# Two cross-attention layers on one core: the probability product in one run, two-chunk steps and a third context buffer in the masked layer

## The chip, the cores and the metric

The kernel runs on one core of one Trainium2 chip. The metric is the device time of that core in microseconds (us), and lower is better. Most executions of one kernel agree within 0.3%.

## The reference

A gated decoder block with two layers works on 32 batches of 56 query tokens (width 128), which attend to 1500 context rows each. Cut to what matters:

```python
x = x + tanh(g_xattn[0]) * diff_attention(layernorm(x), ctx, ctx, ...)  # 32 heads of 4, softmax(q k) v, a1 - lam * a2, rms per head
x = x + tanh(g_ffn[0])   * moe_ffn_0(layernorm(x))                       # 8 experts, top 2, and a shared one
x = x + tanh(g_xattn[1]) * attention(layernorm(x), ctx, ctx, mask, ...)  # 16 heads of 8, masked keys
x = x + tanh(g_ffn[1])   * moe_ffn_1(layernorm(x))                       # 8 gated experts, top 2
```

Only the two attention layers are touched by the change.

## The kernel before

`attend` (L490) runs once per layer: layer 0 (`L0`, 32 heads, no mask) and layer 1 (`L1`, 16 heads, mask). The 32 batches follow one another. The 1500 keys of a batch are cut into 12 chunks of 125 keys, and the kernel takes one **step** per chunk. All engines have an order written out by hand, in which the batches overlap: while batch n is weighed, the maximum is searched for n+1 and n+2, values are projected for n+2, and keys for n+3 (`LEAD`).

On TensorE (PE) a step holds these pieces of work.

- **Scores**, `scores` (L941): keys against queries of one chunk into the PSUM tensor `score_ps[0]` or `[1]` (two banks each). In layer 0 a step has two halves of 896 columns, "place 0" and "place 1", and each half has its own `score_ps`. The halves swap places from step to step (`halves_of`), so that place 0 of a step uses the same `score_ps` as place 1 of the step before. In layer 1 a chunk has 896 columns in all, and the chunks alternate between the two; two matmuls at L962 put the mask in first.
- **Pairs**, `search` (L927): two matmuls of 112 x 500 scores, from which VectorE (DVE) takes a row maximum (`reduce_piece`, L1119). They rotate through three PSUM rooms: `spare_ps`, `max_ps[0]`, `max_ps[1]`. Layer 0 has 48 pieces in a batch (two pairs a step), layer 1 has 24 (one pair a step).
- **The product**, `weigh` (L973): probabilities times values into `acc_ps`, as eight float32 matmuls of 32 output partitions each; four stand side by side in the array. It works on the step before. In layer 0 it is split into two halves of four, with other work between them, except at step 0. In layer 1 the two halves stand together.
- **Preparations**, `use` (L883): T (turn the context), K (project a third of the keys), V (project a third of the values), M (turn the maxima), F and A (turn the output and its normalised form). The table `where` gives the step of each. In layer 0 they write into the `score_ps` that place 0 of the step has used; in layer 1 they take their turn in the three rooms of the pairs.

The order in a step of layer 0 is scores 0, pair 0, scores 1, first half of the product, pair 1, preparation, second half. In layer 1 it is scores, pair, product, preparation. A preparation is copied out by ScalarE (ACT, `drain`, L1038; M of layer 1 by DVE). ACT also takes the exponential of each 125 x 896 scores (`exps`, L1069) and copies the output of a batch out (`copy_output`, L1078).

**SyncE (SP)** issues all transfers, in this order for batch n:

```python
fill_k(n + 2)      # L682: 6 loads of key parts into the key stack of n+2
load_q(n + 3)      # L660: 6 small loads
next_mask(n + 3)   # L712, layer 1
next_context(n + 4)
fill_m(n + 1)      # L693: 4 small transfers of the split maxima, after M
store_k(n + 3)     # L676: 2 stores of the projected keys, from khl to k_parts
```

`fill_k` waits for the two stores of its batch to land and for the scores of the batch that used the slot (three slots). The context of layer 1 has two buffers (`context_parts`, L303), and `next_context` waits until the values of batch n+2 are projected. The search of batch n+2 begins five steps before the end of batch n (`AHEAD`).

**GpSimd (POOL)**: `prepare` (L763) builds the query stack and turns the mask into the two forms that the scores (`mask_f`) and the search (`mask_add`) need; `finish` (L810) normalises the output; `split_keys` (L799) splits the projected keys into two float16 parts.

Of the kernel before, what the change touches and what calls it, by code (L numbers as in the profile page):

```python
# [48 lines left out]
class Layer:  # L49

    def __init__(self, name, heads, hd, masked):
# [12 lines left out]
        self.uses_f = 2  # L64
# [55 lines left out]
def build(nc, a, out):  # L120

    ctx = ExitStack()
    with ctx:
# [132 lines left out]
        for L in (L0, L1):  # L256
            T[f"{L.name}_mask_loaded"] = sem(f"{L.name}_mask_loaded")
            T[f"{L.name}_context_loaded"] = [sem(f"{L.name}_context_loaded{i}") for i in range(1 + L.masked)]
# [44 lines left out]
def context_parts(T, i):  # L303

    return T["ctx_f"][:, i, 0:SK].bitcast(F16).rearrange("p (a k) -> p a k", a=2)


def load_context(sp, T, L, n):

    loaded = T[L.name + "_context_loaded"]  # L310
    if L.masked:
        sp.dma_start(context_parts(T, n % 2), T["ctx_dram"][n:n + 1, :, :, :].rearrange("b d a k -> (b d) a k")).then_inc(loaded[n % 2], 16)
# [177 lines left out]
def attend(T, L):  # L490
# [14 lines left out]
    GD, GC, H = L.group_dims, L.group_cols, L.halves  # L505
# [7 lines left out]
    ctxT = [context_parts(T, 0), context_parts(T, 1) if L.masked else  # L513
            T["kstack"][2][:, K_WORDS:K_WORDS + 2 * SK].rearrange("p (a k) -> p a k", a=2)]
# [41 lines left out]
    LAST, LAST_THIRD = NKT - 1, NTHIRD - 1  # L556
# [11 lines left out]
    if L is L0:  # L568
        where = {("T", 0): (1, 1), ("F", 0): (2, 1), ("T", 1): (3, 1), ("F", 1): (4, 1), ("T", 2): (5, 1), ("K", 0): (6, 1),
                 ("M", 0): (7, 1), ("V", 0): (7, 1), ("K", 1): (8, 1), ("V", 1): (9, 1), ("K", 2): (10, 1), ("A", 0): (11, 1),  # L570
                 ("V", 2): (11, 1)}
# [6 lines left out]
    per_step = L.pieces // NKT  # L578
    assert per_step * NKT == L.pieces
    AHEAD = 5  # L580
    early = AHEAD * per_step
    turnaround = [("F", i) for i in range(L.uses_f)] + [("A", 0)]
# [8 lines left out]
    def at_step(n, t, side):  # L591

        return [(kind, n + LEAD[kind], i) for (kind, i), place in where.items()
                if place == (t, side) and 0 <= n + LEAD[kind] < B]

    def searched(n, t, k):


        if 2 * k >= per_step:
            return []  # L600
        d, place = (1, early + t * per_step) if t < NKT - AHEAD else (2, (t - NKT + AHEAD) * per_step)
# [4 lines left out]
    for n in range(B):  # L606
        for t in range(NKT):
            middle, last = at_step(n, t, 1), at_step(n, t, 2)
            spare_uses += middle + last
            if H == 2:  # L610
                in_scores.update({user: n * NKT + t for user in middle})
                middle = []
            order += searched(n, t, 0) + middle + searched(n, t, 1) + last
# [6 lines left out]
    def halves_of(step):  # L620

        return (0, 1) if step % 2 == 0 or H == 1 else (1, 0)

    def room(user):
# [3 lines left out]
        if user in in_scores:  # L628
            return score_ps[halves_of(in_scores[user])[0]][:, int(user[0] in "MA"), :]
# [15 lines left out]
    with nc.Block() as block:  # L645

        @block.sync
        def _(sp):
# [23 lines left out]
            def store_context(n):  # L672
                sp.wait_ge(s_cp, low_part(n, LAST_THIRD))
                sp.dma_start(T["ctx_dram"][n:n + 1, :, :, :].rearrange("b d a k -> (b d) a k"), ctxT[n % 2]).then_inc(s_cst, 16)
# [7 lines left out]
            def fill_k(n):  # L682
                at_least(sp, s_scores, (n - 2) * NKT * H)
# [18 lines left out]
            def next_context(n):  # L702
# [3 lines left out]
                if L.masked:  # L706
                    at_least(sp, s_v, NTHIRD * (n - 1))
# [797 lines left out]
```

## Time and profile before

| what | value |
|---|---|
| median of 3 runs | 2349.78 us (2349.38 to 2350.72) |
| profiled execution, its own time | 2345.43 us |
| its span, first to last instruction | 2343.1 us |
| mean granted TensorE clock | 0.953 |
| PE busy | 2179.4 us (93%) |
| PE weight loads | 1297.5 us (55%) |
| DVE busy | 1677.4 us (72%) |
| ACT busy | 1507.4 us (64%) |
| POOL busy | 1278.7 us (55%) |
| DMA | 227.82 MB, mean 97 GB/s |

The attention of layer 0 runs from about 140 to 1220 us, that of layer 1 from about 1480 to 2170 us; between and behind them are the feed-forward layers. PE is busy nearly all of the time in both attention layers, but a busy PE is not PE at its peak: matmuls overlap, and the end of each is modelled. So the cost of a piece of work is read here from start to start: the start of the next piece less its own.

### The profile page before, as it was taken

The numbers are of one execution on the slowest core, as the hardware profiler recorded it, in microseconds if no ns is written. First come the engines' busy times: TensorE is split into PE (matmuls) and PEld (weight loads), VectorE is DVE, ScalarE is ACT, GpSimd is POOL, SyncE is SP. The second block draws the span as 40 slices with busy tenths as digits, with TensorE's granted clock in tenths as the row PEclk, the third lists the DMA queues.
The fourth block names the chain that finished last, engine by engine and source line by source line (L and its number), as shares of the span: only waits on it lengthen the run. The fifth ranks groups of instructions, "written<-read, shape, count | busy, mean of one in ns | idle before, by whom it ended". The sixth has DMA issues, their size and how long they took to land. (4 is left out here: it accounts for less than half of the span.)

```text
span 2343.1 us, 67447 instructions
## 1 busy us (share of the span) xinstructions
PE 2179.4 (93%) x27256; PEld 1297.5 (55%) x27256; DVE 1677.4 (72%) x3701; ACT 1507.4 (64%) x2133; POOL 1278.7 (55%) x1418
## 2 busy tenths in 40 slices
PE   3799999999999999999976967999999999999798
PEld 2255555555555555555535853666665666666576
DVE  3688888888888888888825455777776677775644
ACT  2177787787787787787773322677676667667322
POOL 5335555555655655655423445677776777772332
PEclk9599999999999999999997985999999999999799
DMA  3635344344344344344201018576665666661100
GB/s 102 130 75 117 89 100 115 89 103 114 88 103 113 94 100 111 97 98 110 48 2 64 24 35 158 126 143 148 137 140 128 136 137 138 146 124 36 55 1 16
DMA packets 95245, 227.82 MB, mean 97 GB/s; under 512 B 46308, under 2 KB 58852, under 8 KB 88292
## 3 DMA queue, kind: packets, MB, share of 16 engines
q1 hardware_dynamic: 94692, 223.67, 42.3%
q8 instruction: 210, 3.44, 0.7%
q14 instruction: 87, 0.71, 0.1%
q10 hardware_dynamic: 256, 0.00, 0.0%
HBM read 146.77 MB, written 76.48 MB: 95 GB/s over the span
## 5 line engine op out<-in xcount | busy, mean ns | idle before, releaser
L1075 ACT ACTIVATE probs<-score_ps 125x896 f32<-125x896 f32 x1152 | 1014.2, 915 | 203.3 <-PE score_ps L968 200.9
L1133 DVE TENSOR_REDUCE max_part<-max_ps 112x1 f32<-112x500 f32 x1024 | 654.3, 668 | 115.2 <-PE spare_ps L937 66.9
L984 PE MATMUL acc_ps<-probs,vext 125*32 125x224 f32 (+1 forms) x12288 | 670.7, 316 | 2.7 <-issue 2.1
L937 PE MATMUL max_ps<-kstack,qstack 48*112 48x500 f16 x1535 | 507.1, 405 | 4.7 <-DVE max_part L1133 2.6
L968 PE MATMUL score_ps<-qstack,kstack 50*125 50x224 f16 (+1 forms) x6144 | 453.6, 243 | 15.7 <-ACT probs L1075 13.9
L968 PEld LDWEIGHTS score_ps<-qstack,kstack 50*125 50x125 f16 x6144 | 343.1, 134 | 181.1 <-issue 120.2
L1130 DVE CUSTOM_DVE_ANT_0 kstack<-max_ps,kstack 112x500 f32<-112x500 f32 x511 | 335.2, 675 | 127.1 <-PE max_ps L937 75.0
L1133 DVE TENSOR_REDUCE max_part<-spare_ps 112x1 f32<-112x500 f32 x512 | 343.1, 670 | 64.3 <-PE max_ps L937 64.3
L984 PEld LDWEIGHTS acc_ps<-probs,vext 125*32 125x32 f32 x12288 | 260.8, 109 | 220.1 <-issue 151.0
L937 PE MATMUL spare_ps<-kstack,qstack 48*112 48x500 f16 x769 | 310.0, 403 | 19.2 <-issue 15.8
L937 PEld LDWEIGHTS max_ps<-kstack,qstack 48*112 48x112 f16 x1535 | 173.2, 128 | 142.7 <-issue 77.7
L806 POOL CAST khl<-kstack 128x500 f16<-128x500 f32 x189 | 112.9, 598 | 226.7 <-ACT kstack L1054 143.9
L1130 DVE CUSTOM_DVE_ANT_0 kstack<-spare_ps,kstack 112x500 f32<-112x500 f32 x257 | 173.5, 675 | 87.2 <-PE max_ps L937 75.2
L808 POOL TENSOR_TENSOR khl<-kstack,khl 128x500 f16<-128x500 f32 x189 | 201.8, 1068 | 15.3
L1459 POOL TENSOR_TENSOR kstack<-kstack,probs 112x512 f32 (+1 forms) x68 | 90.5, 1331 | 171.3 <-DVE probs L1406 171.2
L823 POOL TENSOR_TENSOR heads_out<-turned,rden 56x64 f32<-56x64 f32 x192 | 55.2, 288 | 216.9 <-DVE rden L1116 206.8
L962 PE MATMUL score_ps<-kstack 56*125 56x448 f16 x768 | 157.8, 401 | 0.2 <-issue 0.2
L777 POOL TENSOR_SCALAR kstack<-mask_in 112x1500 bf16<-112x1500 uint8 x31 | 147.1, 4746 | 2.6
L774 POOL TENSOR_SCALAR kstack<-mask_in 120x1500 f16<-120x1500 uint8 x31 | 147.6, 4762 | 0.0
L937 PEld LDWEIGHTS spare_ps<-kstack,qstack 48*112 48x112 f16 x769 | 98.7, 128 | 82.1 <-issue 60.4
L1058 ACT ACTIVATE vext<-score_ps 125x512 f32<-125x512 f32 x102 | 60.9, 597 | 76.7 <-PE score_ps L911 76.2
L766 POOL TENSOR_TENSOR qstack<-qrows,wide 112x896 f16<-112x896 f16 (+1 forms) x64 | 83.5, 1305 | 47.0 <-DMA qrows<-q_parts 24.8
(200 smaller groups left out, 2688.3 us busy)
## 6 DMA issues: line engine op xcount, KB each, us to landing
kstack<-k_parts SPq DMA_DIRECT2D x384, 187.5 KB, 6.6
k_parts<-khl SPq DMA_DIRECT2D x128, 375.0 KB, 2.7
ctx_f<-in_ctx SPq DMA_DIRECT2D x32, 750.0 KB
ctx_f<-context_parts SPq DMA_DIRECT2D x32, 750.0 KB, 4.5
context_parts<-ctx_f SPq DMA_DIRECT2D x16, 750.0 KB, 3.7
context_parts<-kstack SPq DMA_DIRECT2D x16, 750.0 KB, 3.5
mask_in<-in_mask SPq DMA_DIRECT2D x128, 82.0 KB
qrows<-q_parts SPq DMA_DIRECT2D x384, 7.0 KB, 7.0
```

The lines of the kernel that those rows point to most:

```text
L774: nc.gpsimd.tensor_scalar(by_chunk(mask_f[n % SLOTS][0:HALF + SQ, :]), turned_keys(mask_in[0:HALF + SQ, :]), -BIG, None, ALU.mult).then_in ...
L777: nc.gpsimd.tensor_scalar(by_chunk(mask_add[n % SLOTS]), turned_keys(T["mask_in2"][:, :]), -BIG * BIG, None, ALU.mult).then_inc(s_add, 1)
L806: nc.gpsimd.tensor_copy(khl[:, 0, k], key_f[:, k]).then_inc(s_kp, 1)
L808: nc.gpsimd.tensor_tensor(khl[:, 1, k], key_f[:, k], khl[:, 0, k], ALU.subtract).then_inc(s_kp, 1)
L937: nc.tensor.matmul(room(("P", n, p))[0:PIECE, 0:TK], qstack[n % SLOTS][rows, c, PIECE * i:PIECE * (i + 1)], kstack[n % SLOTS][rows, c, TK ...
L962: nc.tensor.matmul(buf[0:KT, r, 0:448], mask_f[n % SLOTS][HALF * r:HALF * r + SQ, keys], big_eye[HALF * r:HALF * r + SQ, :], start=True, s ...
L968: last = nc.tensor.matmul(buf[0:KT, r, GC * k:GC * (k + 1)], kstack[n % SLOTS][rows, h * here + k, keys], qstack[n % SLOTS][rows, h * here ...
L984: last = nc.tensor.matmul(acc_ps[32 * j:32 * j + 32, TT * S * i:TT * S * (i + 1)].rearrange("p (s c) -> p s c", s=S), vext[n % SLOTS][:, t ...
L1075: nc.scalar.activation(probs[t % 2][:, 896 * h:896 * h + 896].rearrange("k (b c) -> k b c", b=2), score_ps[(t * H + h) % 2][0:KT, :, 0:448 ...
L1130: nc.vector.tensor_tensor_reduce(masked_scores[p % 2], scores, mask_add[n % SLOTS][:, TK * third:TK * third + TK], 1.0, -3.0e38, ALU.add, ...
L1133: nc.vector.reduce_max(best, scores, AX.X).then_inc(s_red, 1)
L1459: nc.gpsimd.tensor_tensor(k, k, tmp[e % DB][:, :, :], ALU.add).then_inc(s_acc, 1)
```

## The change

- **The product in one run.** `weigh` is no longer halved: all of its matmuls stand together. `order_of` chooses one of three orders of a step. It is "both scores first" where the step before has no preparation other than A or M, "scores apart by a pair" in layer 1 where only the step before has one, and otherwise "scores apart by the product": scores 0, pair 0, product, scores 1, pair 1, preparation. In layer 0 this is so in all steps but step 1, which has both scores first.
- **Layer 1 takes two chunks a step**, so 6 steps a batch: two scores of 896 columns, two pairs, and one product of 16 float32 matmuls over both chunks. It has the waits and the swapping of layer 0. Preparations now go to the `score_ps` of place 0 (`where` gives the bank). F is one piece, not two. Steps 0 and 1 have both scores first, step 5 has scores apart by a pair.
- **Keys ahead of values** in layer 1: F and K0 at step 1, K1 and K2 at step 2, M and V0 at step 3, V1 and V2 at step 4, A at step 5. The search runs three steps ahead (half a batch; it was 5 of 12).
- **A third context buffer** in layer 1, in the room of the normalised tokens `XnT`; `next_context` waits for the values of one batch earlier, and stands behind `fill_m`, right ahead of `store_k`.
- **The mask**: POOL makes `mask_add` first, then `mask_f`, without a wait between them; SP waits for both before it loads the next mask.

```diff
-        self.uses_f = 2
+        self.uses_f = self.halves
+        self.steps = NKT if self.halves == 2 else NKT // 2
...
-    return T["ctx_f"][:, i, 0:SK].bitcast(F16).rearrange("p (a k) -> p a k", a=2)
+    room = T["XnT"][:, 0:SK] if i == 2 else T["ctx_f"][:, i, 0:SK]
+    return room.bitcast(F16).rearrange("p (a k) -> p a k", a=2)
...
-        where = {("V", 0): (0, 2), ("F", 0): (1, 2), ("V", 1): (2, 2), ("F", 1): (3, 2), ("V", 2): (4, 2), ("K", 0): (5, 2),
-                 ("K", 1): (6, 2), ("M", 0): (7, 2), ("K", 2): (8, 2), ("A", 0): (10, 2)}
+        where = {("F", 0): (1, 1), ("K", 0): (1, 0), ("K", 1): (2, 0), ("K", 2): (2, 1), ("M", 0): (3, 1), ("V", 0): (3, 0),
+                 ("V", 1): (4, 0), ("V", 2): (4, 1), ("A", 0): (5, 1)}
...
-    AHEAD = 5
+    per_step = L.pieces // STEPS
+    assert per_step * STEPS == L.pieces
+    AHEAD = 3 if L.masked else 5
     early = AHEAD * per_step
+    ORDERS = {"both scores first": ("scores 0", "scores 1", "pair 0", "weigh", "pair 1", "prepare"),
+              "scores apart by a pair": ("scores 0", "pair 0", "scores 1", "weigh", "pair 1", "prepare"),
+              "scores apart by the product": ("scores 0", "pair 0", "weigh", "scores 1", "pair 1", "prepare"),
+              "pairs apart by preparation": ("scores 0", "weigh", "scores 1", "pair 0", "prepare", "pair 1")}
+
+    def order_of(n, t):
+
+        busy = [any(kind not in "AM" for kind, _, _ in at_step(*place)) for place in ((n, t), (n, t - 1) if t else (n - 1, STEPS - 1))]
+        if not busy[1]:
+            return ORDERS["both scores first"]
+        if L.masked and not busy[0]:
+            return ORDERS["scores apart by a pair"]
+        return ORDERS["scores apart by the product" if L.masked and busy[0] else "scores apart by the product" if busy[0] else "scores apart by the product"]
...
-            return score_ps[halves_of(in_scores[user])[0]][:, int(user[0] in "MA"), :]
+            return score_ps[halves_of(in_scores[user])[0]][:, where[user[0], user[2]][1], :]
...
-                    at_least(sp, s_v, NTHIRD * (n - 1))
+                    at_least(sp, s_v, NTHIRD * (n - 2))
...
+                    sp.wait_ge(s_big, n)
...
                     next_mask(n + 3)
-                    if L.masked:
-                        next_context(n + 4)
                 if n + 3 < B and not L.masked:
                     next_context(n + 4)
                     store_context(n + 3)
                 if n + 1 < B:
                     fill_m(n + 1)
                 if n + 3 < B:
+                    if L.masked:
+                        next_context(n + 4)
                     store_k(n + 3)
...
+                    nc.gpsimd.tensor_scalar(by_chunk(mask_add[n % SLOTS]), turned_keys(T["mask_in2"][:, :]),
+                                            -BIG * BIG, None, ALU.mult).then_inc(s_add, 1)
                     nc.gpsimd.tensor_scalar(by_chunk(mask_f[n % SLOTS][0:HALF + SQ, :]), turned_keys(mask_in[0:HALF + SQ, :]),
                                             -BIG, None, ALU.mult).then_inc(s_big, 1)
-                    pool.wait_ge(s_big, n + 1)
-                    nc.gpsimd.tensor_scalar(by_chunk(mask_add[n % SLOTS]), turned_keys(T["mask_in2"][:, :]),
-                                            -BIG * BIG, None, ALU.mult).then_inc(s_add, 1)
...
-                step = n * NKT + t
-                number = step * H + place
+                step = n * STEPS + t
+                number = step * 2 + place
                 h = halves_of(step)[place]
-                if L.masked:
-                    at_least(pe, s_exp, number - 1)
-                elif place == 0:
+                if place == 0:
...
-                buf = score_ps[(t * H + h) % 2]
-                keys = slice(KT * t, KT * t + KT)
+                buf = score_ps[h]
+                chunk, columns = (t, range(h * 2, h * 2 + 2)) if H == 2 else (2 * t + h, range(PAIRS))
+                keys = slice(KT * chunk, KT * chunk + KT)
...
+            def weigh(n, t):
+
+                pe.wait_ge(s_exp, (n * STEPS + t + 1) * 2)
+                if t == 0:
+                    at_least(pe, s_os, n)
+                    pe.wait_ge(s_v, NTHIRD * (n + 1))
+                chunks = [(t, 0)] if H == 2 else [(2 * t + h, 896 * h) for h in range(2)]
+                for chunk, column in chunks:
+                    for i in range(2):
+                        for j in range(4):
+                            u = 4 * i + j
+                            moving = probs[t % 2][:, column:column + S * 896].rearrange("k (s c) -> k s c", s=S)[:, :, TT * u:TT * u + TT]
+                            last = nc.tensor.matmul(
+                                acc_ps[32 * j:32 * j + 32, TT * S * i:TT * S * (i + 1)].rearrange("p (s c) -> p s c", s=S),
+                                vext[n % SLOTS][:, chunk, u, :], moving, start=(chunk == 0 and i == 0), stop=(chunk == NKT - 1),
+                                skip_group_check=True)
+                last.then_inc(s_av, 1)
...
-                    scores(n, t, 0)
-                    search(searched(n, t, 0))
-                    if H == 2:
-                        scores(n, t, 1)
-                    for i in range(2):
-                        if i == 1 and (t or H == 1):
-                            search(searched(n, t, 1))
-                            for user in at_step(n, t, 1):
+                    for work in order_of(n, t):
+                        if work in ("scores 0", "scores 1"):
+                            scores(n, t, int(work[-1]))
+                        elif work in ("pair 0", "pair 1"):
+                            search(searched(n, t, int(work[-1])))
+                        elif work == "weigh" and weighed[0] >= 0:
+                            weigh(*weighed)
+                        elif work == "prepare":
+                            for user in at_step(n, t):
                                 use(user)
-                        if weighed[0] >= 0:
-                            weigh(*weighed, i)
-                    if t == 0 and H == 2:
-                        search(searched(n, t, 1))
-                    for user in at_step(n, t, 2):
-                        use(user)
-            for i in range(2):
-                weigh(B - 1, LAST, i)
+            weigh(B - 1, LAST)
```

## Rows read from the trace of the kernel before

**Rows 1.** Stretches of one batch in each layer: length, busy time of engines (instructions), clock, DMA share, GB/s

```profile
609.08:644.09 35.01, 34.84 (x406) 18.68 (x404) 29.61 (x52) 27.94 (x39) 19.66 (x30) 1.00 0.43 102
1701.71:1724.03 22.32, 22.29 (x391) 14.04 (x388) 16.13 (x54) 15.62 (x23) 16.44 (x13) 1.00 0.65 141
```

**Rows 2.** Source line 925 (one A per batch), layer 0: min/median/max ns, first and last start

```profile
L925 PE MATMUL score_ps<-wide,attn_n x28: 211/212/214, 189.0 to 1134.2; 56*128 56x56 f32 x28
```

**Rows 3.** Timeline of PE, layer 0: start us, us, work [idle before it]

```profile
611.39 0.96 PE L984 MATMUL acc_ps<-probs,vext 125*32 125x224 f32 x16
612.28 0.41 PE L937 MATMUL max_ps<-kstack,qstack 48*112 48x500 f16 x1
...
612.87 0.41 PE L968 MATMUL score_ps<-qstack,kstack 50*125 50x224 f16 x4 [0.17 <-ACT probs L1075]
...
624.50 0.41 PE L968 MATMUL score_ps<-qstack,kstack 50*125 50x224 f16 x4
624.74 0.37 PE L937 MATMUL max_ps<-kstack,qstack 48*112 48x500 f16 x1
...
624.96 0.35 PE L968 MATMUL score_ps<-qstack,kstack 50*125 50x224 f16 x4
625.24 0.59 PE L984 MATMUL acc_ps<-probs,vext 125*32 125x224 f32 x8
625.76 0.54 PE L937 MATMUL max_ps<-kstack,qstack 48*112 48x500 f16 x2
626.23 0.65 PE L895 MATMUL score_ps<-wide,ctx_f 125*128 125x125 f32 x4
626.81 0.59 PE L984 MATMUL acc_ps<-probs,vext 125*32 125x224 f32 x8
```

**Rows 4.** Timeline of ACT, layer 0, across the turn of a batch

```profile
611.09 1.73 ACT L1075 ACTIVATE probs<-score_ps 125x896 f32<-125x896 f32 x2 [0.26 <-PE score_ps L968]
...
613.32 1.73 ACT L1075 ACTIVATE probs<-score_ps 125x896 f32<-125x896 f32 x2
```

**Rows 5.** Timeline of PE, layer 1

```profile
1704.80 0.91 PE L911 MATMUL spare_ps<-w_parts,ctx_f 128*125 128x128 f16 x12
1705.63 0.40 PE L962 MATMUL score_ps<-kstack 56*125 56x448 f16 x2
...
1706.10 0.38 PE L937 MATMUL max_ps<-kstack,qstack 48*112 48x500 f16 x2
1706.40 0.59 PE L984 MATMUL acc_ps<-probs,vext 125*32 125x112 f32 x16
...
1714.76 0.81 PE L904 MATMUL spare_ps<-ctx_f,w_parts 128*128 128x500 f16 x3
```

**Rows 6.** Timelines of DVE and of SP's queue, layer 1: M, its transfers, a fill

```profile
1719.70 0.26 DVE L1106 TENSOR_SCALAR max_rows<-spare_ps 8x112 f16<-8x112 f32 x1
...
1703.46 3.34 SPq L689 DMA_DIRECT2D kstack<-k_parts  x6
...
1720.28 2.44 SPq L699 DMA_DIRECT2D qstack<-max_rows  x4
```

**Rows 7.** DMA issues, layer 1: count, KB each, median us to landing

```profile
k_parts<-khl SPq DMA_DIRECT2D x54, 375.0 KB, 2.8
ctx_f<-context_parts SPq DMA_DIRECT2D x26, 750.0 KB, 4.5
```

**Rows 8.** Source line 689 (the fills), 1600 to 1750 us

```profile
DMA to landing us min/median/max: 3.6/6.6/9.4
```

**Rows 9.** Timeline of SP's queue, start of layer 1

```profile
1424.72 0.92 SPq L679 DMA_DIRECT2D k_parts<-khl  x2
1433.95 2.63 SPq L689 DMA_DIRECT2D kstack<-k_parts  x6
```

**Rows 10.** A gap on PE in layer 1 (timeline), and stretches behind it (as rows 1)

```profile
1831.14 0.67 PE L968 MATMUL score_ps<-qstack,kstack 50*125 50x112 f16 x7 [1.76 <-issue]
...
1831.20:1834.60 3.40, 3.40 (x30) 1.56 (x32) 1.28 (x4) 0.98 (x2) 0.00 (x0) 0.50 0.84 268
1834.60:1838.00 3.40, 3.40 (x62) 1.87 (x62) 1.99 (x6) 2.85 (x4) 2.27 (x3) 1.00 0.05 17
```

More of the change, by code:

```diff
@@ L504, in attend @@
     layer = 0 if L is L0 else 1
-    GD, GC, H = L.group_dims, L.group_cols, L.halves
+    GD, GC, H, STEPS = L.group_dims, L.group_cols, L.halves, L.steps
     K_WORDS = PAIRS * SK
@@ L589, in attend, with at_step @@
     LEAD = {"T": 3, "K": 3, "V": 2, "M": 1, "F": -1, "A": -1}
-    def at_step(n, t, side):
-        return [(kind, n + LEAD[kind], i) for (kind, i), place in where.items()
-                if place == (t, side) and 0 <= n + LEAD[kind] < B]
+    def at_step(n, t):
+        return [(kind, n + LEAD[kind], i) for (kind, i), (step, _) in where.items()
+                if step == t and 0 <= n + LEAD[kind] < B]
     def searched(n, t, k):
-        if 2 * k >= per_step:
-            return []
-        d, place = (1, early + t * per_step) if t < NKT - AHEAD else (2, (t - NKT + AHEAD) * per_step)
+        d, place = (1, early + t * per_step) if t < STEPS - AHEAD else (2, (t - STEPS + AHEAD) * per_step)
         return [("P", n + d, place + 2 * k + r) for r in range(2)] if n + d < B else []
@@ L606, in attend @@
     for n in range(B):
-        for t in range(NKT):
-            middle, last = at_step(n, t, 1), at_step(n, t, 2)
-            spare_uses += middle + last
-            if H == 2:
-                in_scores.update({user: n * NKT + t for user in middle})
-                middle = []
-            order += searched(n, t, 0) + middle + searched(n, t, 1) + last
+        for t in range(STEPS):
+            spare_uses += at_step(n, t)
+            in_scores.update({user: n * STEPS + t for user in at_step(n, t)})
+            order += searched(n, t, 0) + searched(n, t, 1)
     order += [(kind, B - 1, i) for kind, i in turnaround]
@@ L963, in scores @@
                                          big_eye[HALF * r:HALF * r + SQ, :], start=True, stop=False, skip_group_check=True)
-                here = PAIRS // H
-                for k in range(here):
+                for k, c in enumerate(columns):
                     for r in range(2):
                         rows = slice(HALF * r, HALF * r + KROWS + 2)
-                        last = nc.tensor.matmul(buf[0:KT, r, GC * k:GC * (k + 1)], kstack[n % SLOTS][rows, h * here + k, keys],
-                                                qstack[n % SLOTS][rows, h * here + k, :], start=not L.masked, stop=True,
+                        last = nc.tensor.matmul(buf[0:KT, r, GC * k:GC * (k + 1)], kstack[n % SLOTS][rows, c, keys],
+                                                qstack[n % SLOTS][rows, c, :], start=not L.masked, stop=True,
@@ L1084, in _ @@
             for n in range(B):
-                for t in range(NKT):
-                    for h in range(H):
-                        exps(n, t, h)
+                for t in range(STEPS):
+                    for place in range(2):
+                        exps(n, t, place)
                     if t == 0 and n:
                         copy_output(n)
-                    for user in at_step(n, t, 1) + at_step(n, t, 2):
+                    for user in at_step(n, t):
                         drain(user)
@@ L1164, in _ @@
             for n in range(B):
-                for t in range(NKT):
+                for t in range(STEPS):
                     for user in searched(n, t, 0):
                         reduce_piece(user)
-                    for user in at_step(n, t, 1):
-                        drain(user)
-                    if t == where["F", 1][0] + 1 and n:
+                    if t == where["F", L.uses_f - 1][0] + 1 and n:
                         reciprocals(n)
```

79 lines of the change are left out of this document (32 added, 47 removed).

## The prediction

> **What bounds the kernel now.** I read the stretches of one batch first. In layer 0 a batch takes 35.01 us and PE is busy for 34.84 of it; in layer 1 it takes 22.32 us with PE busy for 22.29, while DVE, ACT and POOL have 12 to 30% to spare [rows 1]. Layer 0 repeats this to a hundredth: 28 A transposes lie between 189.0 and 1134.2 us, 945.2 / 27 = 35.01 apart [rows 2]. So both attention layers are bound by PE's queue, and what counts is the distance from one start to the next on it.
>
> In an ordinary step of layer 0 these distances are, from 624.50 on [rows 3]: scores 0.24, pair 0.22, scores 0.28, half product 0.52, pair 0.47, T 0.58, and again a half product. The same work costs more where its neighbour is of another kind: the pair takes 0.22 between two scores and 0.47 behind a product. The whole product in one run, as step 0 has it already, takes 612.28 - 611.39 = 0.89, against 2 x 0.52 in halves [rows 3]. So a run saves about 0.15. In layer 1 scores take 0.47, the pair 0.30, a V 0.83 [rows 5]; its product of one chunk has the 0.59 of a half product of layer 0, so I price it at 0.52 and two chunks in one run at 0.89. A K lasts 0.81 against V's 0.91, so I give it 0.74.
>
> **The other chain in layer 0: the exponentials.** The first exponential at a batch's turn starts at 611.09 and two take 1.73, so the second starts at 611.96; PE, held by it for 0.17, begins the next scores at 612.87 [rows 3, 4]. That is 0.92 from the start of an exponential to scores in the same PSUM, and from those scores to their exponential it is 613.32 - 612.87 = 0.45. Today this chain has slack, because scores 1 stand right behind pair 0.
>
> **Layer 0, the new order.** PE needs 0.24 + 0.30 (pair ahead of a product, from layer 1) + 0.89 + 0.24 + 0.34 + preparation. The 0.34 is the 0.47 less 0.13, as a pair behind scores does not stagger. With T (0.58) that is 2.59, with K 2.75, with V 2.84. But scores 1 now stand behind the product, 0.24 + 0.30 + 0.89 = 1.43 after scores 0. Their exponential must end before the next scores 0, which use the same PSUM: 1.43 + 0.45 + 0.92 = 2.80. So every step lasts at least 2.80. This is what comes late next, and it takes most of the gain. A batch: step 0 2.80, step 1 (both scores first, PE-bound) 0.24 + 0.24 + 0.30 + 0.89 + 0.47 + 0.58 = 2.72, four steps of T and F 11.20, three of K 8.40, the three with V 2.95 (with M), 2.86 and 2.90 (with A). The sum is 33.83 against 35.01, 1.18 less. DVE is busy for 29.6 us of a batch [rows 1], 88% of 33.83, and covers. 29 batches have all preparations: 34 us less.
>
> **Layer 1, PE alone.** Two scores, two pairs and the product take 0.47 + 0.30 + 0.89 + 0.47 + 0.34 = 2.47. Step 0 2.47; step 1 2.47 + 0.13 + F and K 1.2 = 3.80; step 2 with two K 3.87; step 3 with M and V 3.40; step 4 with two V 4.05; step 5 2.65. The sum is 20.2. Two exponentials (1.73) fit into each step. The rooms of the pairs are no longer shared with preparations. POOL's 16.4 us [rows 1] fit as well.
>
> **Layer 1, the loop through SP.** Here I expect a new wait. The first pair for batch n+2 now comes at step 3, at 2.47 + 3.80 + 3.87 + 0.47 = 10.6 us of the batch, and it needs the filled key stack. The fill waits for the two key stores, these stand behind the maxima's transfers (fill_m) and now right behind the context load, and fill_m waits for M, which comes in step 3 behind that very pair. So the loop closes. From the pair: product and second scores to the second pair 1.66; its matmul (0.38) and two reductions (16.13 us for 24 pieces [rows 1], 0.67 each) to 3.4; M's two copies of 0.26 [rows 6] to 3.9; fill_m's four issues 2.44 [rows 6] to 6.4; the context's issue 0.4 to 6.8. Then the stores. By themselves they land in 2.8 us, at 9.6; if they wait until the context has landed (4.5), at 6.4 + 4.5 + 2.8 = 13.7 [rows 7]. I take 11.2, as the two latencies overlap: only the bytes wait behind each other. That they do wait is seen at the start of the layer, where stores issued at 1424.72 behind other traffic let the fill begin only at 1433.95, 9.2 later [rows 9]. The six fills take 2.6 to 3.3 to issue [rows 6, 9]; the last lands 6.6 to 9.4 after its issue [rows 8], so 9.5 to 12.3 after the first start. I take 10.3. The loop is 11.2 + 10.3 = 21.5 us, above PE's 20.2: PE is held about 1.2 us at step 3 of each batch, and a batch gains 22.32 - 21.5 = 0.8. Over 29 batches with key loads that is 24 us. The bounds of the loop are 19.1 (PE rules then, 20.2) and 26.0.
>
> The Trainium skill, DMA: Bandwidth & Descriptors, section "Queues, rings and completion order", says that on each DMA engine the descriptors of a queue are consumed in ring order. By that rule alone the keys' bytes lie wholly behind the context's; [rows 9] agree, and no row shows this pair of transfers alone.
>
> **Edits costed at nothing.** The third buffer removes a wait that no PE row shows; its transfer is hidden by the fact that K0 of the next batch comes over 6 us after the batch begins. If it were late, K0 at step 1 would wait. Mask order: `mask_add` is ready about 5 us earlier, which the earlier search needs. SP's added wait for `mask_f` stands ahead of fill_m, which waits longer for M anyway. One F instead of two saves a copy on ACT, hidden. The last batches, which have fewer preparations, gain 6 x 0.15 each in layer 1 and about 1 in layer 0: 4 us in all.
>
> **Sum.** 34 + 24 + 4 = 62 us from the profiled execution's 2345.4 gives 2283. The median of the runs is 4.35 us above that execution, so I forecast 2287.
>
> **Rivals.**
> - *Fills in time* (0.20). The stores hardly wait, the loop is under 20.2, and PE sets layer 1: 29 x 1.3 = 38 us more gained, 2250. For it: 2.8 us landing and a lower end of 19.1. Against: [rows 9].
> - *The loop is long, slower than before* (0.14). Context and stores land one behind the other: 13.7 + 10.3 = 24.0 a batch, 1.7 over today's 22.32, 49 us lost, 38 gained elsewhere: 2361. It decides from a loop of 22.32 + 38 / 29 = 23.6. It would be seen as a hold of over 3 us at step 3.
> - *The clock falls at the hold* (0.09). A gap of 1.76 us on PE at 1831.14 was followed by a stretch of 3.4 us at a granted clock of 0.50 (1.2 GHz), in which PE finished 30 instructions against 62 in the next at 1.00 (2.4 GHz) [rows 10]. If the 1.2 us hold does the same, each batch loses 1.7: 29 x 1.7 = 49, 2336. The Trainium skill, TensorE: Matmul & The Clock Gate, section "HAM oscillation", holds that short gaps between bursts leave the clock up, which would make this rival cost nothing. The trace shows a fall behind a gap of 1.76 [rows 10], so the measurement decides and the rival stays.
> - *No gain in layer 0* (0.15). If scores to exponential to scores takes 0.12 longer behind a product than at the turn of a batch, a step of 2.80 becomes 2.92 and the gain of 34 is gone: 2321.
>
> **How the numbers follow.** The forecast, with its own spread of about 2270 to 2305, has 0.42. The range 2245 to 2345 takes in the forecast, the fills in time, the clock and the dead layer 0, and leaves out the long loop and the tails. About 0.2% is what a measurement of this kernel can tell from no change (5 us). Only the long loop, and a part of the clock case, are slower: 0.83 faster, 0.03 the same, 0.14 slower.
>
> **What would show it.** In the changed trace: the product of step 2 in layer 0 as one run of 16 in 0.89; scores 1 1.43 behind scores 0; T, F and K steps all 2.80 long, with PE idle behind ACT's exponential at scores 0; a batch of 33.8. In layer 1: a run of 32 in 0.89 (if weight loads bound it, more), a hold at pair 0 of step 3 released by a fill, none at K0, and a batch of 21.5. The forecast is wrong if layer 0's batch is under 33 or above 34.5, or if PE idles in layer 1 at another place, at the first scores for the maxima or at K.

## The result, and the profile after

The changed kernel takes 2421.69 us (median of 3 runs, 2415.97 to 2425.06) against 2349.78: ratio 1.0302, 95% interval 1.027 to 1.0334. It is slower by 72 us, and the forecast was 2287. Layer 0 gained 26 of the 34 us that were foretold. All of the loss is in layer 1.

The page of the changed kernel (its profiled execution took 2415.97 us): span, busy times, TensorE's clock in 40 slices, and two DMA issues (both layers; KB each, median us to landing):

```profile
span 2414.1 us, 67374 instructions
...
PE 2091.1 (87%) x27256; PEld 1294.3 (54%) x27256; DVE 1704.7 (71%) x3701; ACT 1498.2 (62%) x2101; POOL 1272.8 (53%) x1418
...
PEclk9589999999999999999979859988998899999799
...
k_parts<-khl SPq DMA_DIRECT2D x128, 375.0 KB, 4.6
ctx_f<-context_parts SPq DMA_DIRECT2D x22, 750.0 KB, 5.5
```

PE is busy for 88 us less in a span 71 us longer: it now waits. The page takes both layers together. In layer 1 alone the key stores land in 6.6 us (below) where they took 2.8, and the context in 5.4 where it took 4.5 [rows 7].

**Layer 0.** One batch (columns as in [rows 1]), then PE's timeline of a step with F (L933) up to the start of the next, and the step's two exponentials on ACT:

```profile
609.00:643.11 34.11, 32.19 (x407) 16.91 (x405) 30.59 (x52) 27.87 (x39) 19.70 (x29) 1.00 0.46 108
```
```profile
611.67 0.41 PE L978 MATMUL score_ps<-qstack,kstack 50*125 50x224 f16 x4 [0.22 <-ACT probs L1081]
611.91 0.38 PE L949 MATMUL max_ps<-kstack,qstack 48*112 48x500 f16 x2
612.22 0.96 PE L995 MATMUL acc_ps<-probs,vext 125*32 125x224 f32 x16
613.11 0.41 PE L978 MATMUL score_ps<-qstack,kstack 50*125 50x224 f16 x4
...
613.66 0.62 PE L933 MATMUL score_ps<-wide,out_sb 128*56 128x128 f32 x4
614.53 0.41 PE L978 MATMUL score_ps<-qstack,kstack 50*125 50x224 f16 x4 [0.25 <-ACT probs L1081]
```
```profile
612.12 0.92 ACT L1081 ACTIVATE probs<-score_ps 125x896 f32<-125x896 f32 x1
613.56 0.92 ACT L1081 ACTIVATE probs<-score_ps 125x896 f32<-125x896 f32 x1 [0.53 <-PE score_ps L978]
```

The product runs in 613.11 - 612.22 = 0.89. Scores 1 stand 1.44 behind scores 0, their exponential starts 0.45 later, and the next scores in the same PSUM 614.53 - 613.56 = 0.97 after that. So a step lasts 2.86, with PE idle 0.25 at its end, and a batch 34.11 (35.01 before).

**Layer 1.** The A transposes, one in each batch (25 of them in this window), with the first and the last start; then what PE and SP's queue waited for between 1480 and 2150 us (total, times, longest), and the landing times of the key stores (1500 to 2100 us):

```profile
L937 PE MATMUL score_ps<-wide,attn_n x25: 211/211/211, 1509.3 to 2133.6; 56*128 56x56 f32 x25
```
```profile
PE max_ps L949 <- DMA kstack<-k_parts: 85.9, 25, 4.9
```
```profile
SPq L711 <- DVE max_rows L1114: 207.3, 25, 9.6
SPq L697 <- DMA k_parts<-khl: 134.3, 26, 6.0
```
```profile
DMA to landing us min/median/max: 4.8/6.6/8.7
```

The 27 batches with all their preparations last 24.1 to 27.0 us, 25.9 in the mean, where all but five took 22.32 before. In 25 of them PE is held at the first pair of step 3 until a fill has landed, for 1.0 to 4.9 us. SP itself waits twice: in fill_m for DVE's M (L711), in fill_k for the stores (L697).

One round of this loop, from a held pair to the next, is read in three timelines: PE, DVE (the second of the two copies of M), SP's queue.

```profile
1785.86 0.67 PE L949 MATMUL max_ps<-kstack,qstack 48*112 48x500 f16 x2 [3.54 <-DMA kstack<-k_parts]
1786.46 1.72 PE L995 MATMUL acc_ps<-probs,vext 125*32 125x112 f32 x32
...
1789.44 0.26 PE L928 MATMUL score_ps<-wide,neg_max 112*8 112x112 f32 x1
```
```profile
1791.04 0.26 DVE L1114 SCALAR_TENSOR_TENSOR max_rows<-max_rows,score_ps 8x112 f16<-8x112 f16 x1
```
```profile
1791.32 2.46 SPq L711 DMA_DIRECT2D qstack<-max_rows  x4
1793.83 0.45 SPq L314 DMA_DIRECT2D XnT<-context_parts  x1
1794.33 1.05 SPq L691 DMA_DIRECT2D k_parts<-khl  x2
1800.61 2.99 SPq L701 DMA_DIRECT2D kstack<-k_parts  x6
```

The next held pair begins at 1812.16. The windows show the whole round, the hold ahead of it, and the clock behind the hold:

```profile
1785.86:1812.16 26.30, 21.71 (x387) 15.41 (x387) 15.98 (x53) 15.38 (x21) 17.13 (x14) 0.89 0.62 117
1782.35:1785.85 3.50, 0.00 (x0) 0.00 (x0) 0.00 (x0) 0.94 (x2) 3.34 (x5) 1.00 0.89 111
1785.90:1789.30 3.40, 3.40 (x46) 2.27 (x46) 1.29 (x4) 0.10 (x1) 1.18 (x2) 0.50 0.08 19
1789.40:1797.06 7.66, 7.65 (x154) 6.19 (x154) 5.48 (x18) 6.04 (x8) 1.20 (x2) 1.00 0.28 57
```

PE does nothing for 3.5 us, then runs at 0.50 (1.2 GHz) for 3.4 us: the product of 32 takes 1.65 to the next start, where the next one, at 1.00, takes 0.91. Between 1480 and 2150 us there are 25 such stretches of 3.4 or 6.8 us, 129 us in all (one of 3.4 us before). 22 of them belong to a hold for the fill, three to other idle times of PE. The round adds up like this, beside the terms of the prediction:

| stretch | foretold | measured |
|---|---|---|
| held pair to fill_m | 3.9 | 5.46 |
| fill_m to the stores' issue | 2.9 | 3.01 |
| stores' issue to the fill | 4.4 | 6.28 |
| fill to the next held pair | 10.3 | 11.55 |
| sum | 21.5 | 26.3 |

### The profile page after: what moved, and what is told of

The parts are those of the page before. It is cut to its first block and busy times, and to the rows that moved or that the text cites. A ratio compares the mean times of both kernels' runs of the same rounds, so it can differ in the third digit from the quotient of the medians.

```text
span 2414.1 us, 67374 instructions
## 1 busy us (share of the span) xinstructions
PE 2091.1 (87%) x27256; PEld 1294.3 (54%) x27256; DVE 1704.7 (71%) x3701; ACT 1498.2 (62%) x2101; POOL 1272.8 (53%) x1418
## 5 line engine op out<-in xcount | busy, mean ns | idle before, releaser
L1081 ACT ACTIVATE probs<-score_ps 125x896 f32<-125x896 f32 x1152 | 1039.0, 916 | 419.7 <-PE score_ps L978 414.8
L1139 DVE TENSOR_REDUCE max_part<-max_ps 112x1 f32<-112x500 f32 x1024 | 663.8, 672 | 83.5 <-PE max_ps L949 44.2
L995 PE MATMUL acc_ps<-probs,vext 125*32 125x224 f32 (+1 forms) x12288 | 580.5, 320 | 10.3 <-issue 8.5
L949 PE MATMUL max_ps<-kstack,qstack 48*112 48x500 f16 x1536 | 472.6, 405 | 98.3 <-DMA kstack<-k_parts 93.6
L978 PE MATMUL score_ps<-qstack,kstack 50*125 50x224 f16 (+1 forms) x6144 | 463.1, 252 | 73.2 <-ACT probs L1081 67.9
L978 PEld LDWEIGHTS score_ps<-qstack,kstack 50*125 50x125 f16 x6144 | 314.3, 137 | 314.7 <-ACT probs L1081 247.0
L995 PEld LDWEIGHTS acc_ps<-probs,vext 125*32 125x32 f32 x12288 | 316.0, 113 | 198.6 <-issue 145.5
L949 PEld LDWEIGHTS max_ps<-kstack,qstack 48*112 48x112 f16 x1536 | 155.7, 132 | 142.3 <-DMA kstack<-k_parts 97.5
L1062 ACT ACTIVATE vext<-score_ps 125x512 f32<-125x512 f32 x192 | 114.7, 597 | 74.9 <-PE score_ps L923 60.6
```

The lines of the kernel that those rows point to most:

```text
L949: nc.tensor.matmul(room(("P", n, p))[0:PIECE, 0:TK], qstack[n % SLOTS][rows, c, PIECE * i:PIECE * (i + 1)], kstack[n % SLOTS][rows, c, TK ...
L978: last = nc.tensor.matmul(buf[0:KT, r, GC * k:GC * (k + 1)], kstack[n % SLOTS][rows, c, keys], qstack[n % SLOTS][rows, c, :], start=not L. ...
L995: last = nc.tensor.matmul(acc_ps[32 * j:32 * j + 32, TT * S * i:TT * S * (i + 1)].rearrange("p (s c) -> p s c", s=S), vext[n % SLOTS][:, c ...
L1062: nc.scalar.activation(vext[n % SLOTS][:, THIRD * i:THIRD * i + THIRD, :, :].rearrange("k t u (a e) -> k t (u a) e", a=2)[:, :, :, 0:VD], ...
L1081: nc.scalar.activation(probs[t % 2][:, 896 * h:896 * h + 896].rearrange("k (b c) -> k b c", b=2), score_ps[h][0:KT, :, 0:448], ACT.Exp, sc ...
L1139: nc.vector.reduce_max(best, scores, AX.X).then_inc(s_red, 1)
```

## The experiments

**Theories.** *Bytes*: the context's 750 KB ahead of the stores delay their landing, and this closes the loop over PE's 20.2. *Place*: it is SP's order and its wait for M, whatever the bytes. *Clock*: the hold would be cheap, and the half clock behind it is what costs. Each edit below is to the changed kernel, unless another is named. The ratios are to the kernel before, measured beside each.

**1. The old layer 1.** Layer 0 as changed, layer 1 as before.

```diff
-        attend(T, L1)
+        attend_old(T, L1)      # attend of the kernel before
```

> The changed kernel with layer 1 as it was before, so only layer 0 has the new order. My theory: layer 0 gains 0.90 us a batch (34.11 instead of 35.01) and all the loss is in layer 1. So about 26 us less than the kernel before: 2323, and batches of 22.3 in layer 1. A rival, that layer 0's new order harms the rest (clock, feed-forward), would give more than 2335.

Measured: 2326.69 us, ratio 0.9885 (0.984 to 0.993); batches 34.11 and, but for five, 22.32. So layer 0 gives 23 to 27 us by the medians (16 to 38 by the interval), which agrees with 29 batches of 0.90 less, and the new layer 1 costs about 95.

**2. The context load ahead of fill_m.**

```diff
                     next_mask(n + 3)
+                    if L.masked:
+                        next_context(n + 4)
...
                     fill_m(n + 1)
                 if n + 3 < B:
-                    if L.masked:
-                        next_context(n + 4)
                     store_k(n + 3)
```

> The changed kernel, in layer 1 the context load back ahead of the maxima's transfers; nothing else. My theory, a loop from the first pair of step 3 through M, the maxima's transfers, the key stores and the fill: the stores are issued 0.5 earlier and do not wait for the context's bytes (about 2 us), so a batch of layer 1 falls from 26.3 to about 24 and the time from 2422 to about 2355. The rival, that the fills are slow because the traffic is bunched, expects the same batch of about 26 and 2415 to 2425.

Measured: 2272.31 us, ratio 0.9663 (0.9624 to 0.9701); measured again: 2274.93, 0.9678 (0.9654 to 0.9701).

> The kernel with only the context load moved (the best so far, 2272.31) again, in five rounds beside the kernel before and the other two of this call: 2268 to 2280, layer 0's batch 34.11, layer 1's 20 to 22.

This one edit gives back 147 us and beats both kernels. SP's queue and PE over one round (each pair is the first of step 3), PE's wait, and the stores' landing:

```profile
1801.05 0.38 SPq L314 DMA_DIRECT2D ctx_f<-context_parts  x1
1803.27 2.45 SPq L711 DMA_DIRECT2D qstack<-max_rows  x4
1805.76 0.91 SPq L691 DMA_DIRECT2D k_parts<-khl  x2
1808.83 4.18 SPq L701 DMA_DIRECT2D kstack<-k_parts  x6
```
```profile
1799.36 0.42 PE L949 MATMUL max_ps<-kstack,qstack 48*112 48x500 f16 x2
...
1819.37 0.38 PE L949 MATMUL max_ps<-kstack,qstack 48*112 48x500 f16 x2
```
```profile
PE max_ps L949 <- DMA kstack<-k_parts: 7.7, 15, 1.5
```
```profile
DMA to landing us min/median/max: 2.5/3.1/4.5
```

From pair to fill_m it is 3.91, as foretold; stores to fill take 3.07 instead of 6.28. The next pair comes 20.01 later and is not held. Batches last 20.8 in the mean, the shortest 19.97, and the half clock is gone but for three stretches, 31 us, behind the last full batches. I had expected 2.3 us a batch; 5.1 came back. The two rounds differ by 6.3 us: 3.2 from stores to fill, 1.55 on PE, which is no longer at half clock, 0.5 for the context's issue and 1.0 from the fill to the pair.

**3. How many bytes.** The load is split by high and low parts, 375 KB each: one ahead of the stores, one behind. In experiment 4 all of it stands behind.

```diff
                     if L.masked:
-                        next_context(n + 4)
+                        next_context(n + 4, (0,))
                     store_k(n + 3)
+                    if L.masked:
+                        next_context(n + 4, (1,))
```

> The changed kernel with the context load of layer 1 split in two of 375 KB: the high parts stay ahead of the key stores, the low parts go behind them. Number and place of the issues ahead of the stores are as in the changed kernel (all behind M), only the bytes ahead of them are halved. Theory (the context's bytes ahead of the stores' bytes delay their landing): from the stores' issue to the fill it takes some 4.7 us, half way between 6.3 and 3.1; the loop gets 1.6 us shorter, layer 1's batch 25.9 becomes 24 to 24.5 in the mean, and the time 2360 to 2385, between the 2305 of the context behind the stores and the 2422 of the changed kernel. Rival (it is the place of the issue, that is, the wait for M and SP's own order, and not the bytes): stores to fill stay at 6 or more, and the time stays within 10 us of 2422.

Measured: 2357.96 us, ratio 1.0032 (1.0017 to 1.0047), 2 us below the range that I gave *bytes* and 64 us below the 2422 near which *place* expects it; batches 23.7 in the mean. The stores' landing (1500 to 2100 us) and PE's wait:

```profile
DMA to landing us min/median/max: 4.3/4.9/5.6
```
```profile
PE max_ps L953 <- DMA kstack<-k_parts: 55.1, 28, 3.0
```

The place of the issues, all behind M, is that of the changed kernel. With 750 KB right ahead the stores land in 6.6 us (median), with 375 in 4.9, with none in 3.8 (experiment 4, the context right behind) or 3.1 (experiment 2, the context 4.7 us earlier). So *bytes* stands, and *place* falls as the cause of the late landing.

**4. The context behind the stores**, with three buffers, and with two (which also brings back the old wait for the values of batch n+2).

```diff
-                    if L.masked:
-                        next_context(n + 4)
                     store_k(n + 3)
+                    if L.masked:
+                        next_context(n + 4)
```

> The changed kernel, in layer 1 the context load behind the key stores instead of right ahead of them; three buffers kept. My theory: what costs is the context's 750 KB between the maxima and the key stores, so this order is about as good as the one with the context behind the mask loads: batch of 20.3 to 21.3, 2265 to 2295. A rival, that the loss comes from the context's bytes being moved in the busy end of the batch at all, wherever they stand, expects 24 us a batch or more and over 2350.

> As f1_context_last, but with the two context buffers of the kernel before and its wait for the values of batch n+2. Theory: K0 comes some 3 us into the next batch, so the load has over 5 us and lands in time; the third buffer is worth at most 1 us a batch, 2265 to 2320. A rival, that without the third buffer the load is late and holds K0, expects a hold at the K matmuls and over 2320.

Measured: 2304.63 us (0.9776, 0.9759 to 0.9792) and 2308.64 us (0.983, 0.9765 to 0.9895). The stores' landing with three buffers (1500 to 2100 us):

```profile
DMA to landing us min/median/max: 2.5/3.8/4.8
```

With three buffers PE waits 16.4 us for the context at K (L916), with two:

```profile
PE score_ps L916 <- DMA ctx_f<-context_parts: 26.1, 23, 3.4
```

The stores now wait for M exactly as in the changed kernel, and still PE is held for the fill only 9 times, 9.6 us in all: the loop is open. Against experiment 2 it loses about 30 us; the context that comes late for K is 16 of them. The third buffer saves waits of 10 us there; in time the two intervals overlap.

**5. The stores ahead of fill_m**, the context behind both.

```diff
+                if n + 3 < B and L.masked:
+                    store_k(n + 3)
                 if n + 1 < B:
                     fill_m(n + 1)
...
-                    store_k(n + 3)
+                    else:
+                        store_k(n + 3)
```

> The changed kernel, in layer 1 the key stores ahead of the maxima's transfers and of the context load. My theory: the loop is open, since the stores no longer wait for M. The stores follow GpSimd's split at about 16 us of the batch, the fill begins near the start of the next batch, and the hold at step 3 is under 1 us; the maxima's transfers come later (about 19 us) and may hold the first scores by about 1 us. Batch of 21 to 22, time 2275 to 2300. The rival (fills slow by themselves) expects a hold of 2 us or more at step 3 and over 2350.

Measured: 2312.79 us, 0.9838 (0.9787 to 0.9889), 13 us over what I expected. And with the context first, then the stores, then fill_m:

> The changed kernel with SP's order in layer 1: masks, context load, key stores, then the maxima's transfers. It removes both the context's and the stores' wait for M. Theory (the loop pair - M - fill_m - stores - fill holds PE): as the stores now wait only for the split of the keys, the loop is open and batches are 20.0 to 20.5, 2255 to 2270. Rival (what counts is that the context's bytes are away from the stores' bytes in time): context and stores now leave together, the stores land 4 to 6 us after their issue, and the maxima's small transfers land late behind them, so that the first scores of a batch wait; batches 21 to 24, 2285 to 2350.

Measured: 2277.17 us, 0.9677 (0.9645 to 0.9709), the stores landing in 2.9 us by its page. The loop is open and nine batches take 19.97, but others up to 24.6, with PE idle where the profile names no releaser. It ends level with experiment 2, and neither theory's time was hit. PE's timeline of one such idle time, then one DMA queue between 1756.7 and 1758.6 us (packets, MB, share of the 16 engines):

```profile
1757.04 0.37 PE L951 MATMUL max_ps<-kstack,qstack 48*112 48x500 f16 x1
1760.08 0.37 PE L951 MATMUL spare_ps<-kstack,qstack 48*112 48x500 f16 x1 [2.67 <-issue]
```
```profile
q8 instruction: 1, 0.02, 6.0%
```

PE stops between the two matmuls of one pair, and the one 16 KB packet on the queue named "instruction" ends at 1758.59, 1.5 us before PE goes on. The program has 211 such packets, one for every 258 matmuls and weight loads. All 14 idle times of this kind over 0.4 us (1480 to 2090 us, 20 us together) end 1.2 to 1.7 us behind the end of such a packet; of PE's other starts about one in ten stands so. So these are very probably waits for PE's own code, which comes late. The kernel of the stores first has 13 of them, 19 us, more than what it missed its range by; that of experiment 2 has seven, 6 us. No run changed these transfers, so the cause is read from the trace and not tested.

**6. The maxima from ACT's queue**, with the context load moved as in experiment 2, so that SP no longer waits for M.

```diff
-                if n + 1 < B:
+                if n + 1 < B and not L.masked:
                     fill_m(sp, n + 1)
...
+                    if L.masked and t == 4 and n + 1 < B:
+                        fill_m(act, n + 1)
```

> The changed kernel, in layer 1 the maxima's four transfers issued by ScalarE after the exponentials of step 4 and the context load behind the mask loads, so that nothing on SP stands between the mask loads and the key stores but their own data. My theory: no hold at step 3, none for the maxima, PE sets the pace: batch of 20.3 to 20.8, clock at 1.00 through layer 1, time 2245 to 2265. The rival expects a hold at step 3 and over 2330. If ScalarE's four issues (2.4 us) delay exponentials, the batch is up to 1 us longer.

Measured: 2453.97 us, 1.0432 (1.0387 to 1.0476). I was wrong by 190 us. ACT's queue, SP's queue, and the first scores of the next batch on PE:

```profile
1805.56 2.45 ACTq L663 DMA_DIRECT2D qstack<-max_rows  x4
```
```profile
1806.96 2.80 SPq L710 DMA_DIRECT2D kstack<-k_parts  x6
```
```profile
1813.36 0.64 PE L973 MATMUL score_ps<-kstack 56*125 56x448 f16 x2 [4.01 <-issue]
```

The stores land in 2.7 us and the fill begins early. But now it begins together with four transfers of 0.9 KB on which the next scores wait. The last of these lands at 1813.27, in the midst of the fill, and PE goes on 0.09 us later. The landing can be told in 22 batches: in each of them PE goes on 0.09 us behind it, and it comes 3.7 to 6.2 us after the last of the four issues, where the same transfers took 1.6 in experiment 2 (2.7 once). The fill's packets take 1.45 us each on a DMA engine. The Trainium skill, DMA: Bandwidth & Descriptors, section "Queues, rings and completion order", says that an engine drains a whole packet of one queue before it turns to another; the trace agrees as far as the late landing goes, and no view here shows the turns. The issues on ACT's queue also delay the last exponentials, as I had feared: PE waits for them 0.9 us in each of 25 batches. The holds moved to another place and brought 25 stretches at half clock again, 157 us.

**7. The clock alone.** Sixteen matmuls whose results are overwritten stand ahead of the wait for the fill, so that PE is not idle there.

```diff
+                    if p == 0 and L.masked and 2 <= n:
+                        wait_for_room(("P", n, p))
+                        for _ in range(16):
+                            nc.tensor.matmul(...)
```

> The changed kernel with 16 more 500-column matmuls on keys and queries that are loaded already, ahead of the wait for the fill at pair 0 of step 3 of layer 1 (written to the pair's own PSUM room and overwritten by it). They keep PE busy for about 3.3 us of the hold. Theory: the hold of 3.5 to 4.9 us makes the granted clock fall to 1.2 GHz for 3.4 to 6.8 us, which makes M later and is worth about 1.7 us a batch in the loop. With them the clock stays at 2.4 GHz and a batch falls from 26.1 to about 24.5: 2365 to 2385. If the clock is only a companion of the hold and the loop is not lengthened by it, the time stays within 2410 to 2430.

Measured: 2399.01 us, 1.0201 (1.0168 to 1.0235). This is 14 us above the range that I gave. The half clock falls from 129 to 37 us and the batch from 25.9 to 25.2. The clock is a part of the loss, about 23 of 95 us, and not its cause. It may be worth more than that: the sixteen take 3.4 us, so where the fill lands sooner they hold the pair themselves. Of *clock* that much stands: PE's part of the loop (pair, product, pair, M) lies right behind the hold.

**8. Layer 0: scores 1 closer**, on top of experiment 2. First in all steps but step 1: scores 0, pair 0, scores 1, product, pair 1, preparation.

```diff
-        return ORDERS["scores apart by the product" if L.masked and busy[0] else "scores apart by the product" if busy[0] else "scores apart by the product"]
+        return ORDERS["scores apart by the product" if L.masked else "scores apart by a pair"]
```

> e2_context_first with one more edit: in layer 0 the second scores stand ahead of the product (scores, pair, scores, product, pair, preparation) in all steps but step 1. Theory: the 2.86 us step is set by scores 1 behind the product, 1.44, plus their exponential and release, 1.42. With scores 1 at 0.46 PE sets the step: T and F about 2.70, K 2.85, V 2.95, step 0 about 2.25; a batch of about 32.6 instead of 34.11, so about 42 us less than e2: 2225 to 2240. The rival, that the new order's gain needs the scores apart, expects 34 to 35 a batch and 2272 to 2295.

Measured: 2346.04 us, 0.9962 (0.9948 to 0.9976), a batch of 36.71, worse than the theory and its rival had it. PE, and ACT's copy of the preparation:

```profile
616.16 0.81 PE L916 MATMUL score_ps<-ctx_f,w_parts 128*128 128x500 f16 x3
616.90 0.41 PE L978 MATMUL score_ps<-qstack,kstack 50*125 50x224 f16 x4
...
617.74 0.41 PE L978 MATMUL score_ps<-qstack,kstack 50*125 50x224 f16 x4 [0.22 <-ACT kstack L1060]
```
```profile
617.00 0.59 ACT L1060 ACTIVATE kstack<-score_ps 128x500 f32<-128x500 f32 x1 [0.95 <-PE score_ps L916]
```

Scores 1 use the PSUM that the preparation of the step before has filled. It was written last and its copy starts at 617.00, so they wait for it, after ACT has idled for 0.95 us. Scores 1 behind the product have that copy behind them: this is what the chosen order bought. Then in step 0 alone, which has no preparation:

```diff
-        ... if busy[0] else "scores apart by the product"]
+        ... if busy[0] else "scores apart by a pair"]
```

> The kernel with the context load first in SP's order, and in layer 0 step 0 (it has no preparation) takes the order scores 0, pair 0, scores 1, product, pair 1. Theory (in layer 0 each step is as long as the distance from scores 0 to scores 1, plus 0.45 to the exponential, plus 0.97 to the next scores 0): with scores 1 only 0.5 to 0.8 us behind scores 0 instead of 1.44, step 0 becomes PE-bound at 2.25 to 2.5 us instead of 2.86; layer 0's batch 34.11 becomes 33.5 to 33.75, 11 to 18 us less in all, so about 2254 to 2262 against 2272. Rival (the wait comes from the copy of the last preparation of step 11, which writes the PSUM tensor that scores 1 need; ScalarE copies it only after the exponential): scores 1 of step 0 wait for it over 0.5 us and nothing is gained, 2272 or a little more.

Measured: 2271.46 us, 0.9653 (0.9627 to 0.9678), a batch of 34.12. Step 0 did shrink, from 2.86 to 637.47 - 635.10 = 2.37 us, but step 1 grew from 2.56 to 3.06. DVE, which reduces each pair:

```profile
636.35 0.67 DVE L1139 TENSOR_REDUCE max_part<-max_ps 112x1 f32<-112x500 f32 x1
637.63 0.68 DVE L1139 TENSOR_REDUCE max_part<-max_ps 112x1 f32<-112x500 f32 x1 [0.61 <-PE spare_ps L949]
638.23 0.67 DVE L1139 TENSOR_REDUCE max_part<-spare_ps 112x1 f32<-112x500 f32 x1
638.81 1.26 DVE L1139 TENSOR_REDUCE max_part<-max_ps 112x1 f32<-112x500 f32 x2
```

DVE idles 0.61 us before step 1, since the second pair comes late in step 0, and then works without a break: the pairs of step 1 wait for it. PE, DVE and ACT are busy for 32.7, 30.5 and 27.8 us of 34.12, and what was gained at one place was taken at the next.

## Why the prediction was wrong

**Layer 0: right.** The product in one run 0.89, scores 1 at 1.44 (1.43), the step bound by the exponential: all seen. The one term off is exponential to scores: 0.97 instead of 0.92, a step of 2.86, a batch of 34.11 instead of 33.83, a gain of 26 us instead of 34. The rival "no gain in layer 0" had this mechanism, at 0.12 instead of the 0.05 that came. No row showed the 0.13 that the prediction took off its second pair; the pair came at 0.30 (613.36 to 613.66) against 0.34, which cost nothing, since the exponential sets the step.

**Layer 1, PE alone: right.** 20.2 foretold; the shortest batches of experiment 2 take 19.97.

**Layer 1, the loop: right in kind, wrong in size, and this is the step that failed.** The place of the hold, its releaser and the chain were as put down. "I take 11.2, as the two latencies overlap" failed: stores to fill took 6.28 instead of 4.4, nearer to the upper bound of 6.9 (13.7 less 6.8), at which they land one behind the other. From the fill to the pair it was 11.55, within its bounds of 9.5 to 12.3, where I took 10.3. With these two alone the round is 24.6, which is the rival "the loop is long" (24.0). The whole round, 26.3, lies above even the upper bound of 26.0, since no bound had the clock in it.

The trace of the kernel before had this pair of transfers already, though behind other traffic: 0.42 us ahead of the stores of [rows 9] a context load is issued. Its time to landing, then that of the two stores:

```profile
DMA to landing us min/median/max: 7.3/7.3/7.3
```
```profile
DMA to landing us min/median/max: 9.2/9.3/9.5
```

The context landed at 1431.6 and the stores 2.3 and 3.0 us later, one behind the other. In the round above they landed 1.6 and 2.6 us behind the context.

**The clock: a rival that was in truth a consequence.** I gave the long loop 0.14 and the fall of the clock 0.09, as alternatives with a price each. But a long loop makes long holds, a fall comes with nearly all of them (22 of 25), and PE's share of the loop runs right behind the hold, so the two come together and add up: 5.46 instead of the 3.91 at full clock. Their sum by my own prices is 2361 + 49 = 2410, close to 2422, and no case had it; so the range ended at 2345. The price of one fall was about right (1.55 us in the round above, 1.7 foretold), though experiment 7 gave back only 23 us of the 49; their independence was not. The Trainium skill, TensorE: Matmul & The Clock Gate, section "HAM oscillation", describes a kernel that is throttled again behind each wait for a DMA. The trace agrees for 22 of the 25 holds; the other three lasted 0.96, 2.04 and 2.26 us.

**Edits costed at nothing.** No row shows K waiting for the context in the changed kernel, and F and the mask's order cost nothing that shows. DVE did cover layer 0, by less than I thought (experiment 8). What I did cost at 0.4 us, the context's issue ahead of the stores, is the edit on which all turned: its issue is 0.45 us, and its bytes kept the stores 3.2 us longer.

**Why the range ended too low.** This loop cost nothing up to PE's own time, and then its full length. With stores that land in 3.1 us a batch takes 20.8, with 3.8 it is 21.9 (experiment 4, where part of it is the late context), with 4.9 it is 23.7, with 6.6 it is 25.9. My spread treated it as a term like the others.

## What to carry to other kernels

In a queue's order, price a large transfer by its bytes, not by its issue: whatever stands right ahead of a store that somebody waits for is paid by that waiter, and moving it by one place was worth 147 us here. A dependence that runs in a circle through several engines is a bound like an engine; add it up with the pessimistic landing times, and let each case of a hold include the clock that falls behind it. Where several engines are nearly full, as in layer 0 here, shortening one step may only move the wait, so read all engines over two steps before reordering one.

## What the hardware showed that I had not expected

- Stores of 375 KB each landed in 3.8, 4.9 and 6.6 us with 0, 375 and 750 KB right ahead of them in the same queue.
- Transfers of 0.9 KB landed 1.6 us after the last issue in SP's own queue (experiment 2), and 3.7 to 6.2 us after it from ACT's queue, while a fill with packets of 1.45 us was on its way (experiment 6): the second queue did not let them pass.
- Idle times of PE over 0.4 us for which the profile names no releaser (1480 to 2090 us, all kernels but that of experiment 6) ended 1.2 to 1.8 us behind the end of a 16 KB packet on the queue named "instruction" in 89 of 90 cases. The 1.76 us of [rows 10] are one of them.
- Behind idle times of 3.54 us on PE (and of 1.76, [rows 10]) the clock stood at 0.50 for 3.4 us. Other idle times went either way: in the changed kernel two of 2.04 and 2.26 us had no such stretch, in that of experiment 3 ten of 1.0 to 1.57 us had none, in that of experiment 4 three of 1.06 to 1.52 had one.
